# Raising TensorE's semaphores from a drain instruction in the message steps and the GRU tail

## The reference

```python
edge_mats = (bond_features @ W_bond + b_bond).reshape(-1, d, d)   # 400000 x 32 x 32, from 16 features
h = atom_features
for _ in range(STEPS):                                            # 4
    msg = jnp.einsum('eij,ej->ei', edge_mats, h[nbr])
    agg = jax.ops.segment_sum(msg, dst, num_segments=n_atoms)
    h = _gru_cell(agg, h, W_ih, W_hh, b_ih, b_hh)
```

## Time and profile before

| | us |
|---|---|
| median of the three runs | 27782.18 |
| span of the profiled execution | 33286.7 |
| sort, 936 to 7046 | 6110 |
| four message steps, first to last gather (each) | 4897 to 4901 |
| end of a step and its GRU tail (each) | about 251 |
| second layer's scatter, 27890 to 32680 | 4790 |

### The profile page before, as it was taken

One profiled execution on the slowest core, in us unless ns is written; L12 is line 12 of the kernel. 1 busy time (PEld: TensorE's weight loads), 2 busy tenths in 40 slices (PEclk: granted clock), 3 DMA queues, 4 the chain that ended last, 5 costly groups with the idle time before them and its releaser, 6 DMA issues. The chain is left out here.

```text
span 33286.7 us, 248524 instructions
## 1 busy us (share of the span) xinstructions
PE 12311.8 (37%) x67675; PEld 9311.2 (28%) x67676; DVE 9799.0 (29%) x17458; ACT 4841.4 (15%) x12143; POOL 20140.3 (61%) x20823
## 2 busy tenths in 40 slices
PE   5433334434444434444444444444444441000003
PEld 4222222223333333333333333333333330000003
DVE  8555555532222222222222222212222221000006
ACT  7222222211111111111111111111111110000003
POOL 0444444456666656666656666665666666777772
PEclk7666666667677667776666677666777775555555
DMA  3111111111111111111111111111111111111113
GB/s 147 56 60 60 60 60 60 60 36 25 24 25 25 24 22 25 24 25 25 25 22 25 25 24 25 25 22 24 25 24 25 25 24 35 40 40 40 40 40 79
DMA packets 1804969, 1246.48 MB, mean 37 GB/s; under 512 B 1170117, under 2 KB 1735346, under 8 KB 1780271
## 3 DMA queue, kind: packets, MB, share of 16 engines
q1 hardware_dynamic: 574528, 850.03, 8.4%
q0 software_dynamic: 666016, 324.92, 7.2%
q10 hardware_dynamic: 564300, 70.11, 1.4%
HBM read 957.69 MB, written 285.80 MB: 37 GB/s over the span
## 5 line engine op out<-in xcount | busy, mean ns | idle before, releaser
L1081 POOL DMA_INDIRECT h_rows<-h_table,rec x13680 | 12939.7, 946 | 6987.6 <-issue 4190.7
L1231 PE MATMUL outer<-a_masked,h_by_quarter 128*128 128x136 f32 x27360 | 5353.3, 371 | 11179.8 <-DVE h_by_quarter L1122 9823.8
L1231 PEld LDWEIGHTS outer<-a_masked,h_by_quarter 128*128 128x128 f32 x27360 | 5063.9, 272 | 11661.2 <-issue 11293.4
L855 POOL DMA_INDIRECT edges_by_node<-row,place x3125 | 3001.8, 961 | 3159.4 <-DVE row L784 2245.4
L1277 ACT COPY outer_sums<-outer 128x408 f32<-128x408 f32 x4560 | 2171.4, 502 | 17391.6 <-PE outer L1231 7933.1
L1498 POOL DMA_INDIRECT messages_by_bucket<-ms,ix x3420 | 3621.6, 1059 | 1189.7 <-issue 1168.5
L1115 DVE TENSOR_TENSOR a_masked<-rec,gates 128x2040 f32<-128x2040 f32 x912 | 2073.5, 2274 | 6823.6 <-remote 5115.6
L1122 DVE TENSOR_TENSOR h_by_quarter<-h_rows,gates 128x1920 f32<-128x1920 f32 x912 | 1963.2, 2153 | 6720.6 <-DMA h_rows<-h_table,rec 6671.5
L1207 PE MATMUL msg_psum<-outer_sums,w_bond_blocks 128*128 128x480 f32 x7752 | 3544.3, 604 | 0.0
L1207 PEld LDWEIGHTS msg_psum<-outer_sums,w_bond_blocks 128*128 128x128 f32 x7752 | 1594.8, 217 | 1415.8 <-issue 1415.8
L645 PE MATMUL nextf<-o_hi,o_lo 128*128 128x98 bf16 x3125 | 499.7, 231 | 3359.4 <-ACT next_free L700 1997.0
(11 more groups left out here) (276 smaller groups left out, 11907.3 us busy)
## 6 DMA issues: line engine op xcount, KB each, us to landing
h_rows<-h_table,rec POOLq DMA_INDIRECT x13680
key_row<-source_keys SPq DMA_DIRECT2D x125, 1600.0 KB
rec<-edges_by_node SPq DMA_DIRECT2D x1140, 157.5 KB
low_key_row<-source_low_keys SPq DMA_DIRECT2D x126, 800.0 KB
carry_flags<-carry_flags SPq DMA_DIRECT2D x285, 240.0 KB
mr<-messages_by_bucket SPq DMA_DIRECT2D x220, 264.0 KB, 2.7
messages_by_bucket<-zeros SPq DMA_DIRECT2D x36, 1600.0 KB, 36.7
chunk_sums<-scan_t ACTq DMA_DIRECT2D x912, 60.0 KB
```

The costliest lines, as they stand in the source:

```text
L855: pool.indirect_dma_start(out=r3, out_offset=bass.IndirectOffsetOnAxis(ap=place[b][:, u:u + 1], axis=0), in_=row[b][:, u, :], in_offset=No ...
L1081: pool.indirect_dma_start(out=hb[j][:, u, :], out_offset=None, in_=ht, in_offset=bass.IndirectOffsetOnAxis(ap=rec[j][:, u, W_DST:W_DST + 1 ...
L1231: last = pe.matmul(pt[(j * NB + g) % RING][:, at:at + KC], hq[j % 2][:, u, :, :].rearrange("p q d -> p (q d)"), am[j % 2][:, u, :, :].rear ...
```

## The change

Each of TensorE's five increments in the third stage is taken off the last matmul or transpose in front of it. Behind these stands a drain instruction of TensorE now, which raises the semaphore instead. A drain waits until all earlier instructions of the engine have completed. The five are `s_t` (one for each bank, 5 in a tile), `s_msg` and `s_tr` (one each in a group of four tiles), `s_catt` and `s_gate` (one each in a GRU group). No matmul is added, removed or moved, no wait changes, and the other engines' programs are the same.

```diff
--- before.py
+++ after.py
@@ -1204,17 +1204,17 @@
                                 pe.wait_ge(s_ts, copied)
                                 pe.wait_ge(s_scan, ng + 2)
                             for k in range(K1 * part // GI, K1 * (part + 1) // GI):
-                                last = pe.matmul(pm[:, 0:GW], wb[:, k, :], ts[b][:, k, :], start=(k == 0), stop=(k == K1 - 1))
+                                pe.matmul(pm[:, 0:GW], wb[:, k, :], ts[b][:, k, :], start=(k == 0), stop=(k == K1 - 1))
                             if part == GI - 1:
-                                last.then_inc(s_msg, 1)
+                                pe.drain().then_inc(s_msg, 1)
 
                         def turn_scan(ng, b):
                             pe.wait_ge(s_scan, ng + 3)
                             pe.wait_ge(s_sc, ng + 1)
                             hold(pe)
                             for t in range(GI):
-                                last = pe.transpose(px[0:NT, t, :], sc[b][:, t * NT:(t + 1) * NT], ident_f[:])
-                            last.then_inc(s_tr, 1)
+                                pe.transpose(px[0:NT, t, :], sc[b][:, t * NT:(t + 1) * NT], ident_f[:])
+                            pe.drain().then_inc(s_tr, 1)
 
                         def group(n0, ng, b, i, g_, past):
                             for j in range(GI):
@@ -1228,9 +1228,9 @@
                                     pe.wait_ge(s_ts, n0 * NB + (j * NB + g + 1))
                                     for u in range(g * GPB, (g + 1) * GPB):
                                         at = (u - g * GPB) * KC
-                                        last = pe.matmul(pt[(j * NB + g) % RING][:, at:at + KC], hq[j % 2][:, u, :, :].rearrange("p q d -> p (q d)"),
-                                                         am[j % 2][:, u, :, :].rearrange("p k c -> p (k c)"), start=True, stop=True)
-                                    last.then_inc(s_t, 1)
+                                        pe.matmul(pt[(j * NB + g) % RING][:, at:at + KC], hq[j % 2][:, u, :, :].rearrange("p q d -> p (q d)"),
+                                                  am[j % 2][:, u, :, :].rearrange("p k c -> p (k c)"), start=True, stop=True)
+                                    pe.drain().then_inc(s_t, 1)
                         groups_of_step(pe, s, group)
                         turn_scan(s * NGR + NGR - 2, 1)
                         for part in range(GI):
@@ -1240,14 +1240,14 @@
                             pe.wait_ge(s_agg, s * NG + g + 1)
                             pe.wait_ge(s_ct, s * NG + g)
                             for h in range(GB):
-                                last = pe.transpose(pt[h // 4][0:2 * D + 2, (h % 4) * P:(h % 4 + 1) * P],
-                                                    cat[:, g * GB + h, :], ident_f[:])
-                            last.then_inc(s_catt, 1)
+                                pe.transpose(pt[h // 4][0:2 * D + 2, (h % 4) * P:(h % 4 + 1) * P],
+                                             cat[:, g * GB + h, :], ident_f[:])
+                            pe.drain().then_inc(s_catt, 1)
                             pe.wait_ge(s_ct, s * NG + g + 1)
                             pe.wait_ge(s_pre, s * NG + g)
                             for h in range(GB):
-                                last = pe.matmul(pg[:, h, :], ct[:, h, :], wx[:], start=True, stop=True)
-                            last.then_inc(s_gate, 1)
+                                pe.matmul(pg[:, h, :], ct[:, h, :], wx[:], start=True, stop=True)
+                            pe.drain().then_inc(s_gate, 1)
                     nsteps(pe, step)
 
                 @block.scalar
```

## The result

The changed kernel takes 27888.82 us (median of 5 runs, 27881.61 to 27895.87), the kernel before 27782.18 (27779.33 to 27784.53, 5 runs): the ratio is 1.0038, with a 95% interval of 1.0027 to 1.0049. It is 107 us slower; 27,791 had been forecast, and the time lies 9 us above the range.

A forecast was written before the change was run, and what follows sets the result against it. The prediction took GpSimd's issue of indirect DMAs to bound the timed kernel and hide the loop's drains. It added 44 exposed drains at 0.2 us, +9 us, to 27,782 for 27,791 us, range 27,710 to 27,880.

The forecast's parts named there:

- bound by GpSimd's issue nearly throughout: Whole timed kernel: GpSimd issues one gather each 1.25 us, and late increments are absent from the runs, at 86%.
- something that recording brings in beside indirect DMAs: TensorE's late increments in the profile: recording causes them, at 86%; the profiled span exceeds the runs by 5,504.5 us.
- The sign that I had named for it: Changed kernel's profile: with prompt increments the span falls by up to 2,700 us, runs unmoved, confirming that recording delays them.
- I take 0.2 us: Cost of one drain on TensorE: 0.2 us, within -0.03 to 0.5 us.
- the sign named for it: Changed kernel's profile: matmuls behind a drain start some 0.2 us after the bank before, where they followed without a gap.
- has 3.76 us to spare: Loop of tiles: gather 9 waits for three banks with 3.76 us spare; three drains take 0.6 us of it.
- The scan, the transposes and ScalarE's copies have the same slack, as they feed the next group and not the next gather: Loop of tiles: drains delaying these followers of TensorE stay hidden by GpSimd's issue.
- 44 exposed drains: Step ends and GRU tails: 11 unhidden drains a step, 44 x 0.2 = +9 us (-1 to +22).
- Drains end the lateness: Rival, whole kernel: increments are late in timed runs too and drains cure it; 25,053 us in full, chance 9%.
- A drain waits for the same late completion: Rival, loop of tiles: TensorE stands still instead of working ahead; 500 to 1,800 us slower, about 28,900 us, chance 5%.
- Its second condition: Loop of tiles: the slower rival, chance 5%, also decides once a drain takes over 1.25 us, in whatever way.
- The tail's rival: GRU tails: groups run back to back, a drain costs 0.4 us or more; 148 x 0.45 = +67 us, 27,849 us, chance 6%.

The follow-up runs named there:

- e0: The unchanged kernel run again, for a profile beside that of the changed kernel: 27784.35 us, ratio 1.0000.
- e4: The changed kernel without GpSimd's wait in front of gather 9: 35250.07 us, where the kernel before took 33256.58.
- e6: The kernel before with a bare drain behind each bank, the matmul still raising s_t: 33598.47 us, where the kernel before took 33256.58.
- e7: The kernel before with two drains behind each bank, the second raising s_t: 33675.64 us, where the kernel before took 33256.58.
- e12: The changed kernel with SyncE's carry flags load moved behind the next group's first record load: 27810.42 us, where the kernel before took 27785.69.
- e1: The kernel before with the five banks' drains of s_t alone: 27883.26 us, ratio 1.0036.
- e2: The kernel before with the drains of s_msg, s_tr, s_catt and s_gate alone: 27786.49 us, ratio 1.0001.

## Why the prediction was wrong, point by point

**"bound by GpSimd's issue nearly throughout"** held: 943 and 944 ns a gather, and 13,680 times 1.2483 us make all of the unchanged loops and 99.5% of the changed ones.

**"something that recording brings in beside indirect DMAs"** was wrong for the lateness, though what followed from it held. Late increments belong to an execution: they come with a timed 33,257 us and with 27,784 us don't come at all (in e0's profile gathers wait 2 us in all). The profile was of one kind and the runs of the other; the difference of 5,504.5 us shows that, and I gave it the wrong cause. The sign that I had named for it, a span that falls while the runs stay, could not tell the two causes apart: the changed kernel's span is 5,393 us shorter than that of the profile ahead, and its runs moved by 107. That the runs of the result were all of the prompt kind was luck; in the other kind the kernels with drains took over 300 us more than the one before (e4, e6, e7).

**"I take 0.2 us" for a drain** was too low, and its upper bound of 0.5 too: 0.57 us a drain at the lower clock, and 0.40 at the upper one (a bank of six MATMULs takes 1.17 us, 11108.78 to 11109.95, where twelve without a drain take 1.55). The reasoning (the next product starts in an empty engine) was right, and so was the sign named for it: the gap behind a bank is 0.21 us. But the gap is not the whole price, as the six MATMULs between two gaps take longer too, 1.72 us. The Trainium skill gives a constant of about 183 ns for a single bf16 matmul at the lower clock ("TensorE: Matmul & The Clock Gate", section "Single matmul latency"). I had set it against my 0.2 us; it is a third of the 0.57 us measured here. The clock I had left out altogether.

**Gather 9 "has 3.76 us to spare"**: it is 3.3 us in the median of the undisturbed trace, since the three banks take 4.23 to 4.44 us there and not 3.88. Of these 0.81 us are needed from the third bank's end to the gather (11123.51 to 11124.32), so 2.5 us can be lost. The drains take 1.2 of it. That the drains of a normal tile stay hidden was right: 2.1 us lie between the two in the other tiles, of which 1.3 could still be lost.

**"The scan, the transposes and ScalarE's copies have the same slack, as they feed the next group and not the next gather"** is the step that failed. The scan also releases a load on SyncE, which moved 2.3 us into the landing of the tile's last gather. The rows then land 1.6 us later in the median, and the drains had already used half of the 2.5 us: in 162 tiles both together went over it. Without the collision 78 us of the loss go (e12). I had listed TensorE's followers by their waits on engines and left out what their followers start.

**"44 exposed drains"**: the count was right, the price was not. The ends cost 16.4 us for 36 drains and the tails 2.0 for 8, so 18.4 us for 44, or 0.42 each, against 9 forecast; at the ends part of it is the bond products' clock. Most of it is the banks': with their drains alone (e1) the ends grow by 12.7 us, with all the others alone (e2) by 2.2.

**The rivals.** Drains end the lateness: refuted, as no execution was faster, and where increments are late, drains hold TensorE (e4, e6, e7). A drain waits for the same late completion: true of those executions, not of the normal ones. Its second condition, the point from which gather 9 waits, was put at 1.25 us a drain, with the spread on time; with the collision 0.57 was enough. The tail's rival (148 exposed drains): refuted, as the groups follow some 9 us apart (9332.13 to 9341.43, 9.3 us, for VectorE's line 1165 in the last two groups of the changed kernel's first step) and not 6.17, near the 8.7 us that seven sums take, and the tails grew by 2.0 us.

## What to carry to other kernels

Where a change makes an engine later, follow everything that its followers release, the transfers on other queues too, and ask what these will land beside: here a load moved by 2 us cost more than the work that moved it. Take slack from a trace whose span equals the timed runs, and compare the two before anything else. An instruction that empties TensorE can cost more than its own time: in the drained banks of this kernel the clock stayed down for the work behind them as well.

## What the runs showed of the hardware

- One kernel has two kinds of execution, at 27,784 and 33,257 us. In the slower kind TensorE's increments are late beside GpSimd's indirect DMAs (ScalarE waits up to 14.2 us for a bank), and prompt in the last stage, which has none (0.7 us at most). Both kinds came on one and the same chip, at different times. What sets the kind stays open.
- A drain behind six fp32 MATMULs of 128x136 costs TensorE 0.57 us at the lower clock and 0.40 at the upper, and its increment comes within 0.02 us of the last MATMUL's own (1.78 us from a bank's start to its copy against 1.76, medians). A second drain behind it costs 0.09 us.
- Gaps of 0.21 us inside three banks left the clock at its lower level 8.1 us after the first MATMUL; without them it was at the upper level after 4.1 us.
- A gather's rows land in time for a spread 2.4 us after its issue, 4.0 us after it when a load of 240 KB goes out 1.0 to 1.5 us ahead of it, and 4.9 us at less than 0.5 us (medians).
- GpSimd's issue interval is 1.2483, 1.2489 or 1.2504 to 1.2509 us, much the same all through an execution and longer by as much in stages that no drain touches: up to 50 us of the time. What sets it is open, and it limits what a comparison of 0.2% can say.
